# Attention projection in three rounded products, and a residual whose two additions are reordered

## The reference

```
mod = (silu(c) @ wmod).reshape(B, 6, 1, -1); sa, ca, ga, sb, cb, gb = ...
ga, gb: sign kept, magnitude at least 0.25
h = layernorm(x) * (1 + ca) + sa
# attention: phi(u) = exp(u @ omega - |u|^2 / 2) / sqrt(128), 16 heads of 16, causal sums of phi_k v
y = num / den
x = x + ga * (y @ W_proj + b_proj)
h = layernorm(x) * (1 + cb) + sb
# ffn: 4 experts with low-rank parts, the best 2 by softmax
x = x + gb * ffn(h)
```

## Time and profile before

| | us |
|---|---|
| median of 3 runs | 756.73 (754.6 to 759.03) |
| the profiled execution, its own time | 757.15 |
| span of the profiled execution | 754.8 |
| PE busy in the span | 733.7 |
| DVE busy | 516.6 |
| ACT busy | 428.1 |
| POOL busy | 73.5 |
| mean granted TensorE clock | 0.995 of full |

### The profile page before, as it was taken

One profiled execution on the slowest core, in us unless ns is written; L12 is line 12 of the kernel. 1 busy time (PEld: TensorE's weight loads), 2 busy tenths in 40 slices (PEclk: granted clock), 3 DMA queues, 4 the chain that ended last, 5 costly groups with the idle time before them and its releaser, 6 DMA issues.

```text
span 754.8 us, 16910 instructions
## 1 busy us (share of the span) xinstructions
PE 733.7 (97%) x6080; PEld 592.9 (79%) x6080; DVE 516.6 (68%) x1254; ACT 428.1 (57%) x775; POOL 73.5 (10%) x82
## 2 busy tenths in 40 slices
PE   7899999999999999999999999999999999999797
PEld 4678769887788878887698877987788876888466
DVE  6547777577766776677766776757766777656566
ACT  5677455765566636665556655575456655665232
POOL 0560200002000110001000020000200010000200
PEclk9999999999999999999999999999999999999999
DMA  9850570106410273104701065101741028100000
GB/s 309 227 120 2 156 167 15 42 28 196 96 56 0 83 173 64 56 0 131 185 4 56 28 179 113 43 13 35 200 85 56 0 101 190 29 30 3 27 1 29
DMA packets 33929, 62.66 MB, mean 83 GB/s; under 512 B 3694, under 2 KB 17874, under 8 KB 33842
## 3 DMA queue, kind: packets, MB, share of 16 engines
q1 hardware_dynamic: 33334, 61.09, 30.3%
q10 hardware_dynamic: 576, 1.31, 0.5%
HBM read 40.37 MB, written 22.02 MB: 83 GB/s over the span
## 4 chain that ended last, share of the span: by engine, by line
PE 91%; DVE 3%; DMA 2%; ACT 1%; SPq 1%; issue 0%; POOL 0%; ACTq 0%; POOLq 0%; DVEq 0%
PE pa L546 13%; PE ring L679 12%; PE prod L559 8%; PE ring L525 6%; PE pa L421 5%; PE pa L422 5%; PE pa L423 5%; PE ring L579 4%; PE pa L666 4%; PE ring L530 3%; PE ring L768 2%; PE ring L586 2%; PE prod L546 2%; PE ring L701 2%; PE ring L760 2%; PE prod L525 2%
## 5 line engine op out<-in xcount | busy, mean ns | idle before, releaser
L1213 DVE TENSOR_TENSOR am_phk<-pa,const 128x512 f32<-128x512 f32 x112 | 77.0, 689 | 43.5 <-PE pa L546 42.8
L546 PE MATMUL pa<-phq,phkT 128*128 128x128 f32 x768 | 101.3, 275 | 0.0
L546 PEld LDWEIGHTS pa<-phq,phkT 128*128 128x128 f32 x768 | 95.3, 191 | 2.3 <-DVE am_phk L1213 0.2
L1393 DVE SCALAR_TENSOR_TENSOR am_phk<-ring,am_phk 128x512 f32<-128x512 f32 x64 | 44.1, 690 | 47.7 <-PE ring L768 47.7
L525 PE MATMUL ring<-xq,omega_x 100*128 100x512 f32 x198 | 71.1, 439 | 3.2 <-DMA xq<-norm_parts 2.2
L939 ACT ACTIVATE phq<-ring 128x512 f32<-128x512 f32 x84 | 50.6, 602 | 40.2 <-PE ring L525 39.2
L422 PE MATMUL pa<-wo_r,qk_l 128*128 128x256 f32 x248 | 69.7, 281 | 0.0
L421 PE MATMUL pa<-wo_r,qk_r 128*128 128x256 f32 x248 | 69.7, 281 | 0.0
L423 PE MATMUL pa<-wo_l,qk_r 128*128 128x256 f32 x248 | 69.6, 281 | 0.0
L1019 ACT ACTIVATE qk_r<-phq 128x512 fp32r<-128x512 f32 x64 | 40.5, 633 | 49.2 <-DVE phq L1399 49.2
L939 ACT ACTIVATE phkT<-ring 128x512 f32<-128x512 f32 x98 | 58.3, 595 | 13.3 <-PE ring L525 12.9
(11 more groups left out here) (208 smaller groups left out, 1616.1 us busy)
## 6 DMA issues: line engine op xcount, KB each, us to landing
xq<-qk_parts SPq DMA_DIRECT2D x45, 512.0 KB
qk_parts<-qk_r SPq DMA_DIRECT2D x32, 256.0 KB, 4.0
qk_parts<-qk_l SPq DMA_DIRECT2D x32, 256.0 KB, 4.6
xr<-in_L_attn_x SPq DMA_DIRECT2D x8, 512.0 KB, 3.4
out_x<-tg SPq DMA_DIRECT2D x16, 256.0 KB, 2.2
tok<-in_L_attn_x SPq DMA_DIRECT2D x7, 512.0 KB, 3.3
phq<-in_L_wmod SPq DMA_DIRECT2D x2, 512.0 KB, 7.2
am_phk<-in_wi_columns SPq DMA_DIRECT2D x2, 512.0 KB, 8.9
```

The costliest lines, as they stand in the source:

```text
L546: mm = pe.matmul(score_bank(q, a)[:, tt], phkT[:, q % 2, a, tt], query(q)[:, a, tt], start=True, stop=True)
L1213: dve.tensor_tensor(am[:, 2 * (q % 2) + a, :].rearrange("p (c t) -> p c t", c=NT), score_bank(q, a)[:].rearrange("p (c t) -> p c t", c=NT) ...
L1393: dve.scalar_tensor_tensor(r2[:, f % 2, :], z_bank[f % 4][:], 0.0, rho, ALU.max, ALU.mult).then_inc(r2_done.sem, 1)
```

## The change

The projection becomes three fp32r products. `wp_ga` gives way to `wp_r` and `wp_l`, made once before the loop: POOL writes the gated weights in float32 to `wp_gated` (the buffer `tok`), ACT rounds them (`setup_wp`), POOL subtracts (`split_projection`, behind `gate(1)`), and PE and SP wait for that (`wp_low`). `yT` gives way to `yT_r` (ACT, in `y_copy`) and `yT_l` (DVE, new `split_y`). The order of the products changes from token half by token half to k by k. In `residual`, DVE adds the second half behind the first half's `bn_stats`. The POOL copy `mod2_now` is dropped: its readers take their row of `mod2` themselves. Scratch `mk` moves into `s_sb`, the sign scratch of `gate(1)` into `xr`.

```diff
@@ sync, before the loop
-            sp.wait_ge(wp_done.sem, B)
+            sp.wait_ge(wp_low.sem, 1)
@@ tensor
             def projection(n, front_next):
...
-                for half in range(2):
-                    for k in range(KT) if front_next else (1,):
-                        project(n, half, k)
+                if front_next:
+                    project(n, 0, 0)
+                    project(n, 1, 0)
+                project(n, 0, 1)
+                project(n, 1, 1)
 
             def project(n, half, k):
...
-                for t in (2 * half, 2 * half + 1):
-                    mm = pe.matmul(pa[half][:, t % 2 * C:(t % 2 + 1) * C], yT[:, k, t * P:(t + 1) * P], w,
-                                   start=k == 0 and t % 2 == 0, stop=k == KT - 1, skip_group_check=True)
+                wait(pe, yT_high, n, k + 1)
+                for t in tiles:
+                    for w in (w_r, w_l):
+                        pe.matmul(out_of(t), yT_r[k][:, t * P:(t + 1) * P], w,
+                                  start=k == 0 and t % 2 == 0 and w is w_r, stop=False, skip_group_check=True)
+                wait(pe, yT_low, n, k + 1)
+                for t in tiles:
+                    mm = pe.matmul(out_of(t), yT_l[k][:, t * P:(t + 1) * P], w_r,
+                                   start=False, stop=k == KT - 1, skip_group_check=True)
@@ tensor, before the loop
             pe.wait_ge(gates_sb.sem, 2)
+            pe.wait_ge(wp_low.sem, 1)
             pe.wait_ge(ld_low.sem, 16)
@@ scalar, behind features(0, 1) and before the loop
+            def setup_wp():
+                act.wait_ge(wp_done.sem, B)
+                act.activation(wp_r[:], wp_gated, ACT.Copy).then_inc(wp_high.sem, 1)
@@ scalar, y_copy
-                    act.activation(yT[:, k, :], y_bank[k], ACT.Copy).then_inc(yT_done.sem, 1)
+                    act.activation(yT_r[k][:], y_bank[k], ACT.Copy).then_inc(yT_high.sem, 1)
@@ vector
+            def split_y(n, k):
+                wait(dve, yT_high, n, k + 1)
+                dve.tensor_tensor(yT_l[k], y_bank[k], yT_r[k][:].bitcast(F32), ALU.subtract).then_inc(yT_low.sem, 1)
@@ vector, residual (add(b) is the addition of token half b, taken out of the loop)
                 wait(dve, xr_biased, n, 1)
-                for b in range(2):
+                add(0)
+                for b in range(2):
                     wait(dve, x2_step, n, b + 1)
                     for t in (2 * b, 2 * b + 1):
                         dve.bn_stats(stats[:, t, :], xr[:, t, :]).then_inc(ln2_vec.sem, 1)
+                    if b == 0:
+                        add(1)
@@ vector, after_attend
                     split_qk(n + 1, 2)
+                    split_y(n, 0)
+                split_y(n, 1)
                 residual(n)
@@ gpsimd
+            def split_projection():
+                pool.wait_ge(wp_high.sem, 1)
+                pool.tensor_tensor(wp_l[:], wp_gated, wp_r[:].bitcast(F32), ALU.subtract).then_inc(wp_low.sem, 1)
...
             gate_projection()
+            pool.wait_ge(wp_done.sem, B)
             gate(1, gb_rows)
+            split_projection()
             lora_by_expert()
```

More of the change, by code:

```diff
@@ L124, in build @@
         wo_r, wo_l = sb("wo_r", [P, FT, C], F32R), sb("wo_l", [P, FT, C], F32R)
-        wp_ga = sb("wp_ga", [P, B, KT, C])
+        wp_r, wp_l = sb("wp_r", [P, B, KT, C], F32R), sb("wp_l", [P, B, KT, C], F32R)
         low_t = sb("low_t", [P, KT, P])
@@ L136, in build @@
         mod1_now = sb("mod1_now", [P, 2 * KT])
-        mod2_now = sb("mod2_now", [P, 2 * C])
         mod2_cols = sb("mod2_cols", [P, 2 * KT])
-        gb_now, bpg_now = (mod2_now[:, k * C:(k + 1) * C] for k in range(2))
         cT, sT = sb("cT", [P, KT, B]), sb("sT", [P, KT, B])
@@ L168, in build @@
         low_both = norm_r[0:LROWS]
-        mk = sb("mk", [P, NT, LROWS])
+        mk = s_sb[:, :, 0:LROWS]
         route = sb("route", [P, 8, NT, E])
@@ L180, in build @@
         g, rho = phq[:, 1], am[:, 3]
-        yT = phkT[:, 0]
+        yT_r, yT_l = (norm_r, norm_l), (qk_l[:, 3], qk_r[:, 3])
         y = tg[:].rearrange("p b (t c) -> p (b t) c", t=2)
@@ L197, in build @@
         bp_row = tg[:, 1, C:2 * C]
-        half_sign = tok[:, 0:B]
+        half_signs = tok[:, 0:B], xr[:, 0:B]
+        wp_gated = tok[:].rearrange("p (b k) c -> p b k c", b=B)
         ga_rows, wp = xr[:, 0:B], xr[:, B:B + KT]
@@ L232, in build @@
         set_act, mods_ps, gates_ps = sig("set_act"), sig("mods_ps"), sig("gates_ps")
-        wp_done = sig("wp_done")
+        wp_done, wp_high, wp_low = sig("wp_done"), sig("wp_high"), sig("wp_low")
         bias_gated = sig("bias_gated")
@@ L259, in build @@
         last_first = sig("last_first")
-        mod2_set, mod1_set, mod2c_set = sig("mod2_set", 1), sig("mod1_set", 1), sig("mod2c_set", 2)
-        yT_ps, yT_done, prj_ps = sig("yT_ps", 2), sig("yT_done", 2), sig("prj_ps", 2)
+        mod1_set, mod2c_set = sig("mod1_set", 1), sig("mod2c_set", 2)
+        yT_ps, yT_high, yT_low, prj_ps = sig("yT_ps", 2), sig("yT_high", 2), sig("yT_low", 2), sig("prj_ps", 2)
         xr_loaded, xr_biased, x2_step = sig("xr_loaded", 16), sig("xr_biased", 1), sig("x2_step", 2)
@@ L279, in build, with row_of @@
         out_rows = out.rearrange("b (n t p) c -> (b n) p t c", p=P, t=NT)
+        def row_of(mod, n):
+            row = n // BLOCKS_PER_ROW
+            return mod[:, row, :] if isinstance(n, int) else \
+                mod[:, bass.ds(row, 1), :].rearrange("p o c -> p (o c)")
         def block_rows(rows, n):
@@ L655, in projection @@
                     wait(pe, qk_split, n + 1, 2)
-                for half in range(2):
-                    for k in range(KT) if front_next else (1,):
-                        project(n, half, k)
+                if front_next:
[3 more added lines that the diff above has]
+                project(n, 1, 1)
             def project(n, half, k):
                 row = n // BLOCKS_PER_ROW
-                wait(pe, yT_done, n, k + 1)
-                w = wp_ga[:, row, k, :] if isinstance(n, int) else \
-                    wp_ga[:, bass.ds(row, 1), k, :].rearrange("p o c -> p (o c)")
-                for t in (2 * half, 2 * half + 1):
-                    mm = pe.matmul(pa[half][:, t % 2 * C:(t % 2 + 1) * C], yT[:, k, t * P:(t + 1) * P], w,
-                                   start=k == 0 and t % 2 == 0, stop=k == KT - 1, skip_group_check=True)
+                w_r, w_l = (w[:, row, k, :] if isinstance(n, int) else
+                            w[:, bass.ds(row, 1), k, :].rearrange("p o c -> p (o c)") for w in (wp_r, wp_l))
+                tiles = (2 * half, 2 * half + 1)
+                out_of = lambda t: pa[half][:, t % 2 * C:(t % 2 + 1) * C]
+                wait(pe, yT_high, n, k + 1)
[7 more added lines that the diff above has]
+                                   start=False, stop=k == KT - 1, skip_group_check=True)
                 if k == KT - 1:
@@ L952, in attend @@
                 features(n, 3, range(RUN, TILES))
-                act.wait_ge(wp_done.sem, B)
+                act.wait_ge(set_gate.sem, 8)
                 features(n, 4, range(TILES))
@@ L1040, in _ @@
             features(0, 1, range(RUN, TILES), lead=True)
+            setup_wp()
             def after_attend(n, front_next):
@@ L1116, in setup_wa @@
                                           ALU.subtract).then_inc(wa_low.sem, 1)
[L1118 to L1122, removed]
             def aggregate(n, vec, tiles=range(NT)):
@@ L1286, in attend @@
                         split_h(n + 1, hT_r, 2, hT_parts, [1])
+                    else:
+                        split_y(n, 0)
                     advance_state(n, gr)
@@ L1300, in residual, with add @@
             def residual(n):
-                wait(dve, xr_biased, n, 1)
-                for b in range(2):
+                def add(b):
                     wait(dve, prj_ps, n, b + 1)
@@ L1306, in residual @@
                     dve.tensor_tensor(two, pa[b][:], two, ALU.add).then_inc(x2_step.sem, 1)
+                wait(dve, xr_biased, n, 1)
+                add(0)
+                for b in range(2):
                     wait(dve, x2_step, n, b + 1)
@@ L1409, in finish @@
             def finish(n, front_next):
+                gate = row_of(mod2, n)[:, 0:C]
+                dve.wait_ge(set_gate.sem, 8)
                 for b in range(2):
@@ L1416, in finish @@
                         dve.scalar_tensor_tensor(tg[:, t // 2, t % 2 * C:(t % 2 + 1) * C],
-                                                 pa[t // 2][:, t % 2 * C:(t % 2 + 1) * C], w1[:, t:t + 1], gb_now,
+                                                 pa[t // 2][:, t % 2 * C:(t % 2 + 1) * C], w1[:, t:t + 1], gate,
                                                  ALU.mult, ALU.mult).then_inc(scaled.sem, 1)
@@ L1496, in gate @@
             def gate(q, rows):
+                half_sign = half_signs[q]
                 pool.wait_ge(gates_sb.sem, q + 1)
@@ L1516, in gate_projection @@
```

(8 more changed lines are left out.)

## The result

The changed kernel takes 767.38 us (median of 4, 765.58 to 767.92) against 756.95 for the one before: ratio 1.0137, 95% interval 1.0112 to 1.0163. The span of the profiled execution grew from 754.8 to 765.5, or by 10.7.

The account below looks back on a forecast made before the run. PE was taken to bound the blocks, with a DVE, POOL, ACT chain arriving together at the transposes. Start +10.35, blocks +4.2 and end 0 summed to +14.6 us, giving 771.5 us, range 764 to 777.

Parts of the forecast that it names:

- The stall: At the loop entry, PE waits for wp_low from POOL's subtraction and begins 9.2 us later.
- What is given back and the clock: After the loop entry: products no longer waiting for ACT give -0.85 us; a lower clock after idle PE costs +2.0.
- PE's 24 products: Projection in each block: 24 fp32r products at 117.5 ns, 2.82 us, replace eight float32 products of 3.64 us.
- PE's first result late by 0.71: Projection: token half 0 leaves PE later, so DVE's first addition begins at 88.68 instead of 87.97, 0.71 us later.
- DVE's residual: First addition to second neg_mean in a block: 4.20 us instead of 4.40, the second addition filling 0.22 us of idle time.
- Register work: PE's address computation in each block: 0.1 us, bounds 0 and 0.6; as a rival +1.1 a block, 775.2 us, chance 0.13.
- A block: Each of seven loop blocks gets longer by 0.6 us, together +4.2, bounds -0.4 and +1.1 a block.
- Which wait ends last: Before the last two transposes: PE waits for token tile 3 from ACT L981, which comes 0.51 us later, at 94.49.
- blocks gain: Rival on the loop blocks: tile 3 isn't late, PE decides, 0.4 us saved a block, 764.7 us, chance 0.22.
- The last block: End of the kernel: yT splits fall in waiting time and the residual's shape is unchanged; 0, with 0.3 us either way.
- The clock falls in every block: Rival: thinly spaced transposes on PE lower the clock, 1.7 us in each block, 783.6 us, chance 0.06.
- Faster: Rival: the loop-entry wait costs nearly nothing and each block saves 0.82 us, 750.6 us, chance 0.03.

Follow-up runs that it names:

- experiment 2: Changed kernel with ten warm-up products of 128x512 put in front of PE's wait for wp_low: 773.89 us, ratio 1.0207.
- experiment 3: Changed kernel with the projection's products back in the order token half by token half: 762.95 us, ratio 1.0091.
- experiment 4: Changed kernel with the old order in residual, the second half's addition behind the first half's statistics chain: 771.68 us, ratio 1.0187.
- experiment 6: Kernel before the change with only the new order in residual, the second half's addition behind the first half's bn_stats: 756.23 us, ratio 0.9990.
- experiments 5 and 7: Changed kernel with PE's wait for wp_low in the projection and products half by half (754.28 us), or ordered so PE never waits for a remainder (753.98 us).
- experiment 1: Changed kernel with PE's wait for wp_low moved from the loop entry to the projection: 757.9 us, ratio 1.0021.
- experiment 7: Changed kernel with PE's wait for wp_low in the projection and products ordered so PE never waits for a remainder of y: 753.98 us, ratio 0.9959.

## Why the prediction was right in kind and 4.1 us too high

- **The stall** was forecast at 9.2 us and is 9.34. POOL's subtraction took 2.34 us and PE began 0.59 after it, where I had 0.44.
- **What is given back and the clock**: I had -0.85 and +2.0, together 1.15. From PE's first loop product to the last `out_transpose` of block 0 all kernels do the same work: 42.84 us before, 43.26 in the changed kernel, 41.84 in experiment 2 with a stall and full clock. So 1.00 us is given back, ACT being idle and ready, and the low clock takes 1.42 of that again. Net 0.42: the first term that was mis-sized, by 0.7 us. The price of the clock isn't one number. Experiment 3 has the same stall and the same work and takes 44.63 us, experiment 4 takes 43.77; the lower level lasted 6.3 and 4.4 us behind the entry there, against 3.3. That is 2.8 and 1.9 us, so the 2.0 was a fair size, and the changed kernel's profile was a mild case.
- **PE's 24 products**: at 117.5 ns forecast and, once they run, seen: the chain has pieces of four (L676) at 0.47 us. Behind a wait the first pair takes longer (0.50 us at 96.37, where later pairs take 0.24).
- **PE's first result late by 0.71**: seen 0.66. The wait for the first `yT_l` is there in the trace ([0.31 <-DVE] on the weight load at 96.37). That the size fits so well is in part luck: PE resumed at 86.60 by the clock of before, 0.30 earlier than forecast, and the 14 products then took 1.94 us and not 1.65.
- **DVE's residual**: I took out only the 0.22 us of idle time, 4.40 to 4.20. It took 3.95 (98.40 to 102.35). The mis-sized term, the largest in the blocks: the second addition's hand-overs went too. Before, it began after `neg_mean` and statistics waited for it; now `bn_stats` of half 0 is followed by an instruction that doesn't depend on it, and the next one that does starts 0.08 us before the addition ends. Experiment 4 restores the old order and measures it at 0.44 us a block, and 0.45 is what the two traces' difference says.
- **Register work**: I added 0.1 us a block and bounds up to 0.6. The line has the 14 register instructions of before, two a block, and 14 more (ALU_OP) of 32 ns, so what was added is 0.06 us a block at most. The addresses are computed once per k and shared by the four calls. A wait of PE for them doesn't show:

```profile
L676 PEldq FUSED_REGOPS  x14: 56/80/110, 95.4 to 631.1; - x14
L676 PEldq ALU_OP  x14: 32/32/32, 95.6 to 631.2; - x14
```

- **A block** so is +0.275 us and not +0.6. Block 0 has 0.17 from its last `out_transpose` to the cut of block 1 (45.65 us against 45.48), so seven blocks make 1.8 of the 4.2 forecast. This is where most of the miss is.
- **Which wait ends last.** I named tile 3 from ACT L981 (L1000 after). It ends at 103.96 and PE uses it at 104.02, so it ends last. The first six transposes are held too, by the fourth q/k remainder, in the same queue of DVE; my chain lacked this branch, which costs nothing while tile 3 is later. What I had wrong is the start: I read two chains that arrive together, and against the rival "blocks gain" that L981 ends 0.04 us before PE wants it. PE's weight load had been waiting for 0.26 us, so tile 3 was the later one already, and all that delayed it went into the block.
- **The last block**: forecast 0, seen -0.89. Before, PE's four router products (L701) ran at the lower clock level, here (L715) at full. From the timeline of the kernel before:

```profile
716.29 3.56 PE L701 MATMUL ring<-am_phk,low_t 128*128 128x512 f32 x4 [0.82 <-ACT am_phk L985]
```

  and from the timeline of the kernel after:

```profile
727.65 1.98 PE L715 MATMUL ring<-am_phk,low_t 128*128 128x512 f32 x4 [0.82 <-ACT am_phk L1004]
```

  That is 1.58 us less, and PE's last product comes as much sooner behind them. Of it 0.9 us are lost again at the very end, in the last transfer of `out_x`. The two transfers of the last block, issue to landing, before and after:

```profile
DMA to landing us min/median/max: 2.2/2.3/2.4
```

```profile
DMA to landing us min/median/max: 2.2/2.7/3.3
```

  The last one is the slow one: 2.4 us in the kernel before and in experiment 6, 3.2 or 3.3 in all seven profiles with the new projection; why stays open. The statistics aren't late here: the second `neg_mean` ends 8.19 us behind the last `out_transpose`, against 8.30 before. In all seven profiles with the new projection the four router products of the last block take 1.98 or 1.99, in both with the old one (experiment 6: 3.68) they are slow. Why the clock doesn't fall there stays open: PE waits longer ahead of the transposes now (1.13 against 0.52 us), not less.

The rivals: "blocks gain" was refuted in the changed kernel (89.15 > 88.88), though it is what experiments 5 and 7 do once the order is mended. "Register work" is refuted by the count and by the 32 ns. "The clock falls in every block" didn't happen: the clock is 1.00 over blocks 1 to 6. "Faster" would have needed what experiment 1 did to the wait, and the order of experiment 3 besides.

Summed as I had it, with measured terms: 9.34 at the entry, 0.42 for clock and what is given back, 0.17 + 1.65 in the blocks, -0.89 at the end: 10.7, which is the difference of the spans. Three terms came out below the forecast and none clearly above it, and the stall alone, 9.2 of the 14.6, made "slower" safe.

## What to carry to other kernels

Put a wait for a set-up product at its first use, not where the setup happens to end: here the place of one line was worth 9.5 us of 10.4. Work taken off the engine with the larger busy share gives nothing where that engine waits for another's result (experiment 7), and an edit that does it by delaying that result loses; ask of each product which half is handed on first, and to whom. A gap of 0.02 us in front of a product doesn't say that its engine was on time: read what its weight load waited for. An exchange of two instructions on the second engine was worth 0.44 us a block where its operand was there in time, and 0.10 us of chain where it wasn't.

## What the hardware showed that I had not expected

- The granted clock of the start-up differs between executions. Where PE stood still for 1.70 to 2.18 us from about 28.5 us on (the kernels before and after, experiments 6 and 7), it fell behind that, and the first 16 products of L546 (L551) took 2.71 to 3.05 us. Where it stood still for 0.58 to 1.05 us (experiments 1, 2, 3 and 5) it didn't, and they took 1.79. Experiment 4 doesn't fit: 0.83 us, and 3.12. The slow case costs about 1.3 us.
- After a stall of nine us the lower level lasted into the first 3.3 to 6.3 us of work and cost 1.4, 1.9 and 2.8 us in three profiles, on both sides of the 1.7 us after the short stall in the earlier trace rows.
- The last store of the program took 3.2 or 3.3 us in every profile with the new projection and 2.4 in both without, for the same bytes.
- Ten more products ahead of a loop went with one stall of 3.2 us at its first jump back and nine more packets of instruction fetches; the page names no engine as the cause, and it is one profile. That makes filling a stall with idle products a risk of its own.
